# Four residual graph layers on 1024 nodes: the third-layer Laplacian matrix dropped for scales in the split operands, and batch 1's first layer moved under batch 0's attention

## The reference, cut to what matters

```python
# layer 0
y = einsum('nm,bmf->bnf', adj, x) + x
y = einsum('bnf,fo->bno', y, W0) + b0
x = layernorm(x + y / max(row_norm(y), 1e-12))
# layer 1 (attention)
A = (x @ q) @ (x @ k).T / sqrt(128)
A = exp(tanh(A / 8) * 8) * adj
x = layernorm(x + (A / A.sum(-1)) @ x @ v)
# layer 2
res = si[:, :, None] + sj[:, None, :] + adj * w_r + g_b      # si, sj: x @ w_i, x @ w_j
x = layernorm(x + einsum('bij,bjd->bid', res, x) @ W2 + b2)
# layer 3 (Chebyshev, K = 3)
L = eye - dis[:, None] * adj * dis[None, :]                  # dis = adj.sum(-1) ** -0.5
T2 = 2 * (L @ L) - eye
x = layernorm(x + relu(x @ W30 + (L @ x) @ W31 + (T2 @ x) @ W32 + b3))
```

## Time and profile before

| | before |
|---|---|
| runs | 725.47 us median of 3 (725.03 to 727.37) |
| profiled execution | 725.35 us, span 723.2 us |
| mean granted clock of PE | 0.968 |
| PE busy | 640.1 us (89%) |
| DVE busy | 597.2 us (83%) |
| ACT busy | 385.1 us (53%) |

### The profile page before, as it was taken

The page is one execution under the profiler, slowest core; times in us unless marked ns, Lnnn a source line. Parts: engine busy times, 40 slices in busy tenths (PEclk is TensorE's granted clock), DMA queues, the critical chain, the costliest instruction groups (busy, mean ns, idle before and its releaser), DMA issues. The chain is left out here.

```text
span 723.2 us, 17684 instructions
## 1 busy us (share of the span) xinstructions
PE 640.1 (89%) x7606; PEld 489.1 (68%) x7606; DVE 597.2 (83%) x1495; ACT 385.1 (53%) x531; POOL 72.5 (10%) x49
## 2 busy tenths in 40 slices
PE   5727946889999999999999999998999999869895
PEld 5714623566976698667966697668866796637895
DVE  6667978997989798988989898988889897879525
ACT  3668756743458245934486255914494446613402
POOL 0020011001200120011200120011100220020102
PEclk9959977999999999999999999999999999989998
DMA  8010000000100020001100020002000010000101
GB/s 308 2 29 1 2 16 15 1 1 2 31 1 2 1 60 2 1 2 29 34 1 2 1 61 2 1 2 60 2 1 2 1 31 2 1 1 2 31 2 59
DMA packets 20013, 14.55 MB, mean 20 GB/s; under 512 B 864, under 2 KB 18912, under 8 KB 19936
## 3 DMA queue, kind: packets, MB, share of 16 engines
q1 hardware_dynamic: 18816, 12.91, 5.6%
q10 hardware_dynamic: 1120, 0.52, 0.3%
HBM read 9.24 MB, written 4.19 MB: 19 GB/s over the span
## 5 line engine op out<-in xcount | busy, mean ns | idle before, releaser
L239 POOL TENSOR_TENSOR small<-small,minus_half 128x8 f32<-128x8 f32 x39 | 68.1, 1750 | 636.5 <-DVE small L533 320.9
L387 ACT ACTIVATE att<-r,coef 128x1024 f32<-128x1024 f32 x64 | 70.5, 1102 | 53.5 <-PE r L1115 52.9
L1243 PE MATMUL av<-vhi,p_hi 128*128 128x129 f16 x512 | 89.7, 220 | 9.0 <-DVE p_lo L806 8.7
L1246 PE MATMUL av<-vhs,p_lo 128*128 128x129 f16 x512 | 89.5, 220 | 0.0
L1245 PE MATMUL av<-vlo,p_hi 128*128 128x128 f16 x512 | 89.5, 219 | 0.0
L801 DVE TENSOR_TENSOR att<-att,adjT 128x1024 f32<-128x1024 f32 x64 | 78.0, 1218 | 7.6 <-ACT att L389 7.6
L806 DVE SCALAR_TENSOR_TENSOR p_lo<-p_hi,att 128x1024 f16<-128x1024 f16 x64 | 77.9, 1218 | 0.0
L1113 PE MATMUL r<-gr,lap 128*128 128x128 f16 x448 | 75.8, 219 | 0.0
L1115 PE MATMUL r<-gr,lap 128*128 128x128 f16 x448 | 75.8, 219 | 0.0
L1114 PE MATMUL r<-gr,lap 128*128 128x128 f16 x448 | 75.8, 219 | 0.0
L1115 PE MATMUL r<-xq,lap 128*128 128x128 f16 x448 | 75.4, 219 | 0.0
(11 more groups left out here) (304 smaller groups left out, 1925.8 us busy)
## 6 DMA issues: line engine op xcount, KB each, us to landing
x<-in_x SPq DMA_DIRECT2D x8, 512.0 KB, 4.2
lap<-in_adj SPq DMA_DIRECT2D x8, 512.0 KB, 8.7
out<-outb SPq DMA_DIRECT2D x7, 512.0 KB, 3.5
out<-att SPq DMA_DIRECT2D x1, 384.0 KB, 2.8
...
```

Source lines behind the costliest of these rows:

```text
L239: return nc.gpsimd.tensor_tensor(dst, src, minus_half[:], ALU.pow)
L387: nc.scalar.activation(att[:, s], (r1, r0)[t % 2][:], ACT.Tanh, scale=c_tanh).then_inc(S["th"], 1)
L1243: mm(acc, p_hi[:, s, chunk(j)], vhi[:, t, 0:D + 1], start=(t == 0 and j % 3 == 0), stop=False, skip_group_check=True)
L1246: l_ = mm(acc, p_lo[:, s, chunk(j)], vhs[:, t, 0:D + 1], start=False, stop=(t == C - 1), skip_group_check=True)
```

## The change

- `lap` is gone. `apply_laplacian` reads `a_hi` and `a_lo`, and the row scale `-dis^2` is applied when r and q are split: `r_hi`, `r_lo`, `q_hi`, `q_lo` work chunk by chunk (128 columns), since the scale differs between chunks, where they worked on halves (512 columns). `row_scales` computes the scales once.
- `adj_rows` has its own memory, which after the load holds a second set of x1T, g, vhi, vlo, vhs and the split of r. The residual of layer 0 is written in place into `xas[b % 2]`; batch 1's input is loaded into `outb` at the start.
- The order of the start is written out in `start()` on each engine: the adj loop runs its products two chunks behind its transposes; batch 1's adj product stands ahead of and between batch 0's x1 steps; the rest of batch 1's layer 0 stands between the steps of batch 0's attention; layer norm 1, the x2 split and the gate sums of batch 0 between the steps of batch 1's attention. `front(i)` and `back(i)` for i = 2 to 6 (`back` also for 1) are the old bodies in the old order.

```diff
-R_DOWN = 1.0 / 512
+R_DOWN = 1.0 / 256
 Q_DOWN = 1.0 / 4
 ADJ_UP = 256.0
-LAP_UP = 256.0
 LO_UP = 2048.0
...
-DVE_COPIES = 2
+DVE_COPIES = 1
...
-lap = sb("lap", [P, 2, C, N], F16)
-adj_rows = lap[:].rearrange("p a c n -> p (a c n)").bitcast(F32).rearrange("p (c n) -> p c n", c=C)
+adj_rows = sb("adj_rows", [P, C, N])
+later = adj_rows[:].rearrange("p c n -> p (c n)").bitcast(F16)
+def late(first, size, **dims):
+    inner, = dims
+    return later[:, first:first + size].rearrange(f"p (a {inner}) -> p a {inner}", **dims)
...
+deg, dis, dis2, root_deg, eps_deg, r_scale, q_scale = (sb(n_, [P, C]) for n_ in ("deg", "dis", "dis2", "root_deg", "eps_deg", "r_scale", "q_scale"))
...
-x1 = sb("x1", [P, C, D])
 x1T = sb("x1T", [P, 2, N], F16)
-gr = sb("gr", [P, 2, N], F16)
-vhi = sb("vhi", [P, C, AVW], F16)
-vlo = sb("vlo", [P, C, D], F16)
-vhs = sb("vhs", [P, C, AVW], F16)
+xts = (x1T, late(0, 2 * N, n=N))
+gs = (sb("g", [P, 2, N], F16), late(2 * N, 2 * N, n=N))
+rs = late(4 * N, 2 * N, n=N)
+vhis = (sb("vhi", [P, C, AVW], F16), late(6 * N, C * AVW, w=AVW))
+vhss = (sb("vhs", [P, C, AVW], F16), late(6 * N + C * AVW, C * AVW, w=AVW))
+vlos = (sb("vlo", [P, C, D], F16), late(6 * N + 2 * C * AVW, C * D, d=D))
...
+xas = (sb("xa", [P, C, D]), sb("xb1", [P, C, D]))
...
+def x0_of(b):
+    return outb if b == 1 else x0
...
     def r_hi(z, b, h):
         act.wait_ge(S["r_mm"], 2 * b + h + 1)
-        copy(z.gr[:, 0, half(h)], r2[:, half(h)], R_DOWN).then_inc(S["r_hi"], 1)
+        for j in range(h * C // 2, (h + 1) * C // 2):
+            l_ = copy(z.gr[:, 0, chunk(j)], r2[:, chunk(j)], r_scale[:, j:j + 1])
+        l_.then_inc(S["r_hi"], 1)
...
-        copy(cd(z.xq[:, 0])[:, half_chunks(h)], z.pq[:, half_chunks(h)]).then_inc(S["q_hi"], 1)
...
+        for j in range(h * C // 2, (h + 1) * C // 2):
+            l_ = copy(z.xq[:, 0, chunk(j)], z.pq[:, j], q_scale[:, j:j + 1])
+        l_.then_inc(S["q_hi"], 1)
...
+    def start():
+        y0_hi(0, 1, r1[:, half(1)])
+        degrees(0, 3)
+        act.wait_ge(S["y0_mm"], 2)
+        x0_hi(1)
+        degrees(3, C)
+        act.wait_ge(S["p0_mm"], 2)
+        y0_hi(1, 0, m7[:])
+        norm(0, 0, xas[0], V_CHUNKS)
+        x1t_hi(0, r1)
+        g_hi(0, r2)
+        y0_hi(1, 1, av[:, 2])
+        v_hi(0, r1)
+        v_scaled(0)
+        for t in range(C):
+            exponent(0, t)
+            if t >= 1:
+                p_hi_part(0, t - 1)
+        norm(0, 1, xas[1], V_CHUNKS)
+        p_hi_part(0, C - 1)
+        x1t_hi(1, r0)
+        g_hi(1, r1)
+        v_hi(1, r0)
+        v_scaled(1)
+        for t in range(C):
+            exponent(1, t)
+            if t >= 1:
+                p_hi_part(1, t - 1)
+            if t == 1:
+                norm(1, 0, xas[0], V_CHUNKS)
+                copy_x2(0)
+            if t == 4:
+                bias_rows()
+        p_hi_part(1, C - 1)
+        act.wait_ge(S["p0_mm"], 4)
+        y2_hi(0, 0)
...
-    def lap_scales():
+    def row_scales():
 
         dve.wait_ge(S["dis_ok"], 1)
         tt(dis2[:], dis[:], dis[:], ALU.mult)
-        stt(lap_s[:], dis[:], -LAP_UP / (LO_UP * P_UP), dis[:], ALU.mult, ALU.mult)
+        stt(r_scale[:], dis[:], -R_DOWN, dis[:], ALU.mult, ALU.mult)
+        stt(q_scale[:], dis[:], -1.0, dis[:], ALU.mult, ALU.mult)
         ts(eps_deg[:], deg[:], EPS, None, ALU.mult)
-        tt(root_deg[:], deg[:], dis[:], ALU.mult).then_inc(S["lap_sc"], 1)
-    def lap_lo_part(*rows):
-        for c in rows:
-            dve.wait_ge(S["lap_hi"], c + 1)
-            stt(lap[:, 1, c, :], adjT[:, c, :], lap_s[:, c:c + 1], lap[:, 0, c, :],
-                ALU.mult, ALU.subtract).then_inc(S["lap_lo"], 1)
+        nc.vector.memset(vhis[1][:, :, D:D + 1], 1.0)
+        nc.vector.memset(vhss[1][:, :, D:D + 1], 1.0 / LO_UP)
+        tt(root_deg[:], deg[:], dis[:], ALU.mult).then_inc(S["sc_ok"], 1)
...
     def r_lo(z, b, h):
-        split_lo(z.gr[:, 1, half(h)], r2[:, half(h)], R_DOWN, z.gr[:, 0, half(h)], "r", 2 * b + h + 1)
+        dve.wait_ge(S["r_hi"], 2 * b + h + 1)
+        for j in range(h * C // 2, (h + 1) * C // 2):
+            l_ = stt(z.gr[:, 1, chunk(j)], r2[:, chunk(j)], r_scale[:, j:j + 1], z.gr[:, 0, chunk(j)],
+                     ALU.mult, ALU.subtract)
+        l_.then_inc(S["r_lo"], 1)
...
     def q_lo(z, b, h):
-        hc = half_chunks(h)
         dve.wait_ge(S["q_hi"], 2 * b + h + 1)
-        tt(cd(z.xq[:, 1])[:, hc], z.pq[:, hc], cd(z.xq[:, 0])[:, hc], ALU.subtract).then_inc(S["q_lo"], 1)
+        for j in range(h * C // 2, (h + 1) * C // 2):
+            l_ = stt(z.xq[:, 1, chunk(j)], z.pq[:, j], q_scale[:, j:j + 1], z.xq[:, 0, chunk(j)],
+                     ALU.mult, ALU.subtract)
+        l_.then_inc(S["q_lo"], 1)
...
+    def start():
+        x0_max(1)
+        dve.wait_ge(S["bc_in"], 16 * 7)
+        rows = Rows(0)
+        rows.begin()
+        rows.y_half(0, r1[:])
+        y0_lo(0, 1, r1[:, half(1)])
+        rows.stats_half(0)
+        x0_scale_read(1)
+        x0_scales(1)
+        rows.y_half(1, r1[:])
+        rows.stats_half(1)
+        rows.arg()
+        x0_lo(1)
+        rows.residual()
+        ln_begin(0, 0, xas[0])
+        weights_split(1, 2)
+        ln_shift(0, 0)
+        ln_norm(0, 0, xas[0])
+        y0_lo(1, 0, m7[:])
+        x1t_lo(0, r1)
+        g_lo(0, r2)
+        y0_lo(1, 1, av[:, 2])
+        v_lo(0, r1)
+        rows = Rows(1)
+        rows.begin()
+        mask(0, 0)
+        for t in range(1, C):
+            mask(0, t)
+            p_lo_part(0, t - 1)
+            if t == 1:
+                rows.y_half(0, r2)
+                rows.y_half(1, r2)
+            if t == 2:
+                rows.stats_half(0)
+                rows.stats_half(1)
+                rows.arg()
+            if t == 3:
+                row_scales()
+            if t == 4:
+                rows.residual()
+            if t == 5:
+                ln_begin(0, 1, xas[1])
+            if t == 6:
+                gate_weights()
+                ln_shift(0, 1)
+                ln_norm(0, 1, xas[1])
+        p_lo_part(0, C - 1)
+        x1t_lo(1, r0)
+        weights_split(3, 4)
+        w_ch.end()
+        x0_max(2)
+        g_lo(1, r1)
+        v_lo(1, r0)
+        row_sums(0)
+        for j in range(C):
+            l_ = attention_residual(0, j)
+        l_.then_inc(S["e1a"], 1)
+        x0_scale_read(2)
+        mask(1, 0)
+        dve.wait_ge(S["e1a"], 1)
+        ln_begin(1, 0, xas[0])
+        mask(1, 1)
+        p_lo_part(1, 0)
+        ln_shift(1, 0)
+        ln_norm(1, 0, xas[0])
+        mask(1, 2)
+        p_lo_part(1, 1)
+        x2_lo(0)
+        mask(1, 3)
+        p_lo_part(1, 2)
+        x0_scales(2)
+        sj_ch = Count(dve, S["sj_c"], 0, 5)
+        for k_ in range(2):
+            sj_step(sj_ch, 0, k_)
+        mask(1, 4)
+        p_lo_part(1, 3)
+        for k_ in range(2, 4):
+            sj_step(sj_ch, 0, k_)
+        mask(1, 5)
+        p_lo_part(1, 4)
+        mask(1, 6)
+        p_lo_part(1, 5)
+        mask(1, 7)
+        p_lo_part(1, 6)
+        p_lo_part(1, 7)
+        y2_lo(0, 0)
+        l2_ch = Count(dve, S["l2_c"], 0, L2_LINKS)
+        sums_read(0, m7)
+        sums(0)
+        l2_read(l2_ch, 0, m7)
+        l2_rank_one(l2_ch, z_all, 0)
+        x0_lo(2)
+        return l2_ch
...
-                l_ = split_product(dst[:, chunk(j)], lap[:, 0, m, chunk(j)], lap[:, 1, m, chunk(j)],
+                l_ = split_product(dst[:, chunk(j)], a_hi[:, m, chunk(j)], a_lo[:, m, chunk(j)],
                                    src[:, 0, chunk(m)], src[:, 1, chunk(m)], m == 0, m == C - 1)
...
-        if c == 1:
+        if c == 2:
             pe.wait_ge(S["x_lo"], 1)
             pe.wait_ge(S["iu_ok"], 1)
-        if c == 3:
             pe.wait_ge(S["w_max"], 5)
             mm(m7[:, 3 * P:3 * P + 5], ones[:], wmax[:], start=True, stop=True).then_inc(S["w_sum"], 1)
-        if c >= 1:
-            adj_x0_chunk(c - 1)
-    pe.wait_ge(S["y0_lo"], 1)
-    pe.wait_ge(S["w_red"], 6)
-    project_half(r1, yT, w0s[:, 0], w0s[:, 1], 0).then_inc(S["p0_mm"], 1)
-    adj_x0_chunk(C - 1)
...
+    def start():
+        pe.wait_ge(S["w_red"], 6)
+        layer0_half(0, 0, r1)
+        adj_x0_chunk(C - 1)
+        row_max_sum(1)
+        layer0_half(0, 1, r1)
+        pe.wait_ge(S["x_lo"], 2)
+        adj_x0(0, 0, C, m7, 0)
+        adj_x0(1, 0, 4, av[:, 2], 0)
+        x1_t(0, r1)
+        adj_x0(1, 4, 6, av[:, 2], 0)
+        pe.wait_ge(S["w_red"], 10)
+        g_product(0, r2)
+        adj_x0(1, 6, C, av[:, 2], 0)
+        v_product(0, r1)
+        pe.wait_ge(S["g_lo"], 2)
+        scores(0, 0)
+        pe.wait_ge(S["v_lo"], 2)
+        scores(0, 1)
+        layer0_half(1, 0, r2)
+        layer0_half(1, 1, r2)
+        next_scores(0, 2)
+        next_scores(0, 3)
+        pe.wait_ge(S["e0_c"], 8 + 3)
+        attend(0, 0)
+        for t in range(4, C):
+            next_scores(0, t)
+            attend(0, t - 3)
+        attend(0, 5)
+        pe.wait_ge(S["th"], C - 1)
+        x1_t(1, r0)
```

(114 more changed lines are left out.)

809 lines of the change are left out of this document (317 added, 492 removed).

## The result

| | before | changed |
|---|---|---|
| runs | 725.52 us median of 4 (725.03 to 727.37) | 738.42 us median of 4 (738.23 to 738.64) |
| ratio | | 1.0172, 95% interval 1.0157 to 1.0187 |
| profiled execution | 725.35, span 723.2 | 738.64, span 736.5 |
| second-layer product of batch 0 starts | 159.09 us | 153.47 us |
| distance of the batches | 79.09 us | 81.82 us |

The changed kernel is 1.7% slower. I split the difference of the spans at the same landmark that the prediction uses, PE's second-layer product: the start gives back 5.6 us, six distances cost 16.4 (498.75 us from batch 0's product to batch 6's, against 482.36), the stretch after it 2.5. Together +13.3, which is the difference of the spans, 736.5 - 723.2. The range of 724 to 741 holds the time.

The account below looks back on a forecast made before the run. The prediction saw a start where PE stands still in holes and a middle where PE is nearly full, so each PE delay delays the end. Start -10.6, layer-3 splits +17.1 and tail +2.5 gave +9.0: 734.4 us, range 724 to 741.

Parts of the forecast that it names:

- Steady state: Layer-3 splits of r and q in narrow pieces: 2.85 us a batch, in six batches +17.1 us.
- Tail: After the last batches' bodies, narrow splits of r and q of batch 6 and r of batch 7: +2.5 us (1 to 4).
- Start: Up to batch 0's second-layer product on PE: begins at 148.5 instead of 159.1 us, -10.6.
- It waits once more, for the weight maxima (about 2 us ...): PE in layer 1 of adj: one wait for DVE's 2.3 us of reductions; last chunk product near 31.1, not 33.1.
- DVE's list from the first mask to the last split: Through batch 1's attention: 69.3 us of work, 4.1 of waits and 0.3 for hand-overs, from 60.8 to 134.5 us.
- the eight attends, five scores and four parts of adj_x2: PE work (23 us) after the wait for step 2's tanh: ends 3.4 us later as the clock falls.
- The falls after the gaps at 40 and 110 us: PE's clock in the start: at half near 39 us and near 105 to 115 us.
- Without either clock fall it would be about -15.6: The start's gain if PE's clock did not fall: about -15.6 us instead of -10.6.
- -20: The start's gain with no clock fall and the waits of DVE gone as well: -20 us.
- the two sides cancel: Rival: start of -15.6, ACT's small copies at 0.20 a step, 2.2 us a batch, tail 2: 725.0 us; chance 0.13.
- most of the splits' time is taken up by idle time elsewhere: Rival: only 1 us a batch comes through, with a start of -15.6: 716.8 us; chance 0.10.
- ACT's narrow copies cost as much a step as the norms: Rival: 0.384 a step, 3.9 us a batch, tail 4, start wins only 8: 744.8 us; chance 0.15.

Follow-up runs that it names:

- e1: Changed kernel with the four layer-3 splits of r and q in halves of 512 columns again, degree scales left out: 717.8 us, distance of the batches 79.10.
- e2: Changed kernel with only the two splits of r in halves of 512 columns, their degree scale left out: 727.2 us (one run), distance 80.40.
- e3: Kernel before with its r and q split in pieces of 128 columns, the scale read from a constant column: 744.5 us, distance 81.83.
- e4: Changed kernel with the weight maxima one matrix chunk later on VectorE and their sum two chunks later on TensorE: 731.7 us.
- e7: e6 with idle matmuls in three gaps of TensorE in the start: 716.5 us.
- e5: Changed kernel with idle matmuls in four of TensorE's gaps of the start: 734.0 us.
- e6: e4 with layer 3's degree scale at the matrix product's output, r and q split in halves of 512 without a scale: 716.9 us, distance 79.67.
- e8: e6 with ScalarE's part of batch 0's attention norm and copy of x2 behind the exponent of step 2, not ahead: 713.2 us.

## Why the prediction was right, and where it was not

**Steady state: right.** Distance forecast 81.95, measured 81.82. By landmarks in one batch, counted from the second-layer product: the first Laplacian starts 1.0 us later than in the kernel before and x1's transposes 1.4 (forecast +1.5 for r), the product with g 0.5 more (q's first half, forecast 0.45), the last Laplacian 0.8 more (q's second half, 0.9). ACT's step out of PSUM, the one price with no row, is 0.26 us (7 steps and a last of 0.384 make 2.18); I had taken 0.28 between the ends 0.20 and 0.384. What the Trainium skill says on "VectorE: DVE Perf Modes", section "The TRN2 errata — SBUF-src ops pay a fixed extra latency per instruction", agrees in direction: small tiles pay the fixed cost each, and the trace has q's four copies of 128 columns out of SBUF at 1.28 us where one of 512 took 0.63. The prediction's estimate from its figure, 0.25 us for a PSUM copy of 128 columns, is near the measured step of 0.26, not the duration of 0.384. e1 to e3 show the cause from three sides.

**Tail: right**, 2.5 forecast and measured.

**Start: the step that failed is "It waits once more, for the weight maxima (about 2 us ...)".** It was mis-sized twice. The wait was 4.4 us, because the reductions could not begin when DVE was free: they waited 1.9 us for the weights' DMA. The trace before did hold the hint, a reduction at 15.62 us behind work that covered the wait, but no row showed a wait for it, and I took "DVE's 2.3 us" as the whole price. Then the clock fell in the gap, and the first products ran at half speed until 22.7 us. Together the first tanh came at 63.51 instead of the forecast 58.6, +4.9, and the product at 153.47 instead of 148.5, +5.0: the error arose ahead of the mask and passed on whole. e4 takes that wait away, and the first tanh comes at 56.88 and the product at 146.76.

**Behind the mask: right as a length, by luck.** DVE's list from the first mask to the last split was forecast at 73.7 us and took 74.2 (65.80 to 139.95). Mask to product was forecast at 87.7 and is 87.67, but two errors inside cancel. PE ended the attention 76.6 us after the mask instead of 78.5: the 3.4 us that the prediction put in for the fall of the clock ahead of "the eight attends, five scores and four parts of adj_x2" are not there. PE ended 2.5 us behind DVE's last split, where 1.4 + 3.4 was forecast, and in e7, with the clock at 1.00 in that place, it is 2.5 too. And the stretch after the attention took 11.0 instead of 9.2, of which 1.7 is a fall of the clock that I had not foreseen; at full clock it is 9.35 in six of the runs.

**The clock: half right.** The falls after the gaps at 40 and 110 us came as forecast; those at 16, 91 and 145 us were not forecast. "Without either clock fall it would be about -15.6" does not hold: e5 gives 3.9 us for the two falls ahead of the mask, one of them unforeseen, and e7 against e6 gives 1.4 for the one at 40 us and nothing for the one at 110. What a fall costs depends on whether PE is the engine that the others wait for: ahead of the mask, and again in the last four adj_x2 parts (1.7 us), but not between. That DVE's waits are worth the rest ("-20") is borne out in part: e8 gains 2.8 us between mask and product by ending one of them.

**The rivals.** That most of the splits' time is taken up by idle time elsewhere fell with a distance of 81.82: its sum had 1 us a batch, and 2.73 came. That ACT's narrow copies cost as much a step as the norms fell with 0.26 a step. That the two sides cancel needed both a start of -15.6 and 2.2 a batch; neither came.
